# Scoring the edges of a graph attention layer: products on VectorE in place of turned rows on TensorE, and gathers written out

## The reference, cut to what matters

```python
x_l = (x @ W_l + b_l).reshape(n, H, C)          # H = 8 heads of C = 32
x_r = (x @ W_r + b_r).reshape(n, H, C)
src, dst = (edge_index[0], edge_index[1])       # dst is sorted
x_j = x_l[src]
g = jax.nn.leaky_relu(x_r[dst] + x_j, 0.2)
alpha = jnp.einsum('ehc,hc->eh', g, att)        # the scoring stage computes alpha
alpha = alpha + jnp.log(edge_attr)[:, None]
```

## Time and profile before

| | us |
|---|---|
| median of three runs (lowest, highest) | 5924.41 (5920.71, 5925.23) |
| the profiled execution, its own time | 5924.94 |
| its span, first to last instruction | 5923.2 |
| busy: PE, DVE, ACT, POOL | 4048.7, 2628.5, 1112.7, 3097.9 |
| first instruction of the scoring stage | 244.79 |
| first VectorE instruction of the stage after it | 1547.41 |

### The profile page before, as it was taken

How to read it: one execution, slowest core, us unless ns; L and a number is a source line. 1 busy time by engine, 2 the same in 40 slices (tenths; PEclk the granted TensorE clock), 3 DMA queues, 4 the chain that set the end, 5 groups by cost and what they waited for, 6 DMA issues and landing times. The chain is left out here.

```text
span 5923.2 us, 82263 instructions
## 1 busy us (share of the span) xinstructions
PE 4048.7 (68%) x19460; PEld 3300.3 (56%) x19461; DVE 2628.5 (44%) x5923; ACT 1112.7 (19%) x2524; POOL 3097.9 (52%) x3161
## 2 busy tenths in 40 slices
PE   4788999999469965089934555555455555592998
PEld 3577888888447744067734444444444444461665
DVE  5333333333689975034444434444433334342443
ACT  0122222222159921022210000000000000021121
POOL 1166767676248831500066777777677777603111
PEclk9889888888679985599955556666555555555999
DMA  5365555565248843342242111111211111122220
GB/s 197 94 183 182 180 178 181 177 181 177 70 157 273 272 135 108 122 125 64 62 122 54 32 32 33 33 33 30 44 33 32 33 32 34 28 72 81 84 79 31
DMA packets 414884, 602.72 MB, mean 102 GB/s; under 512 B 97612, under 2 KB 305118, under 8 KB 413351
## 3 DMA queue, kind: packets, MB, share of 16 engines
q1 hardware_dynamic: 283019, 348.08, 17.8%
q0 software_dynamic: 107056, 200.91, 14.7%
q10 hardware_dynamic: 24732, 52.87, 2.6%
HBM read 392.17 MB, written 221.97 MB: 104 GB/s over the span
## 5 line engine op out<-in xcount | busy, mean ns | idle before, releaser
L1867 POOL DMA_INDIRECT big<-t_d,src_tiles x1564 | 1497.9, 958 | 552.2 <-issue 462.5
L2090 PE MATMUL v_bank<-big,v_oh 128*128 x3328 | 682.9, 391 | 926.4 <-POOLq L1863 861.6
L2090 PEld LDWEIGHTS v_bank<-big,v_oh 128*128 128x128 f32 x3328 | 649.6, 299 | 1004.0 <-issue 1004.0
L640 POOL DMA_INDIRECT se_xj<-xl_d,se_idx x832 | 833.8, 1002 | 371.9 <-issue 193.0
L1945 DVE TENSOR_TENSOR big<-big,v_bank 128x64 f32 x1664 | 367.8, 221 | 1158.0 <-PE v_bank L2090 922.8
L737 PE MATMUL se_z_ps<-big,se_oht 128*128 x1664 | 543.4, 455 | 73.1 <-issue 45.7
L683 DVE TENSOR_TENSOR se_z<-se_z_ps,se_xj 128x528 f32<-128x528 f32 x416 | 293.3, 705 | 584.8 <-DMA se_xj<-xl_d,se_idx 450.3
L976 POOL TENSOR_TENSOR ae_v<-ae_v,ex 128x1792 f32<-128x1792 f32 x104 | 334.2, 3217 | 243.0 <-DMA ae_v<-xj_d 242.8
L759 PEld LDWEIGHTS se_al_ps<-atta,se_zt 128*128 128x128 f32 x3328 | 459.3, 214 | 0.0
L759 PE MATMUL se_al_ps<-atta,se_zt 128*128 128x8 f32 x3328 | 444.5, 260 | 0.0
L1017 PE MATMUL ae_bank<-ae_v,ae_oh 128*128 128x266 f32 x1664 | 401.1, 396 | 51.4 <-DVE big L1001 37.4
(11 more groups left out here) (406 smaller groups left out, 5916.6 us busy)
## 6 DMA issues: line engine op xcount, KB each, us to landing
xj_d<-se_xj SPq DMA_DIRECT2D x208, 528.0 KB, 3.4
ae_v<-xj_d SPq DMA_DIRECT2D x208, 528.0 KB
big<-t_d,src_tiles POOLq DMA_INDIRECT x1564
buf_d<-e_blank ACTq DMA_DIRECT2D x4, 4112.0 KB, 35.7
e_xs<-buf_d SPq DMA_DIRECT2D x106, 128.0 KB
y_d<-e_y SPq DMA_DIRECT2D x106, 128.0 KB
se_xj<-xl_d,se_idx POOLq DMA_INDIRECT x832, 3.1
v_xt<-xnt_d SPq DMA_DIRECT2D x98, 128.0 KB
```

The costliest lines, as they stand in the source:

```text
L640: nc.gpsimd.indirect_dma_start(half_of(u)[:, k, :], None, table, bass.IndirectOffsetOnAxis(ap=idx[:, u, k:k + 1], axis=0)).then_inc(landed ...
L1867: nc.gpsimd.indirect_dma_start(rows[:, t % RING, :], None, table, bass.IndirectOffsetOnAxis(ap=m.srct[:, t:t + 1], axis=0)).then_inc(lande ...
L2090: last = nc.tensor.matmul(bank[u][:, k * MH:(k + 1) * MH], oh[:, u, k, :], of_block(rows, at[k]), start=True, stop=True)
```

## The change

The scoring stage is rewritten in these parts:

- the leaky ReLU is split as 0.2 z + 0.8 max(z, 0). The folded linear columns take 0.2, and `att` times 0.8 lies in SBUF once for each partition (`attb`).
- VectorE computes w = max(z, 0) * attb for a pair (`weigh`, one instruction of 512 elements a partition), sums w over each head's 32 (`total`, 16 sums), and adds the linear columns once a group.
- TensorE no longer turns z and no longer multiplies by att.
- the one-hots are made on ScalarE, as max(0, 1 - |iota - dl|): eight instructions and one more for a group.
- the turned one-hots have two PSUM tiles in place of one.
- the gathers are written out: no loop, no copy of indices and no wait for it. The index column comes straight from `m.src`.
- the gathered rows lie in the free part of `big1`.

```diff
-        idx = sb("idx", [P, 4, HS], U32)
-        xj = sb("xj", [P, 2, GS, LW])
+        xj = m.big1[:, CL:CL + 2 * GS * LW].rearrange("p (u k d) -> p u k d", u=2, k=GS)
...
-                def gather(h, u, r):
-                    if at_least(h, 4):
+                for h in range(2 * NG):
+                    u, r = h % 4, h // 4
+                    if h >= 4:
                         pool.wait_ge(landed[u], 16 * HS * r)
                         pool.wait_ge(s["z_ready"], 2 * h - 6)
                         pool.wait_ge(stored[u], 16 * r)
-                    nc.gpsimd.tensor_copy(idx[:, u, :], m.src[:, bass.ds(h * HS, HS)]).then_inc(s["indexed"], 1)
-                    pool.wait_ge(s["indexed"], h + 1)
-                    pool.sem_inc(s["issued"], 1)
                     for k in range(HS):
+                        t = h * HS + k
                         nc.gpsimd.indirect_dma_start(half_of(u)[:, k, :], None, table,
-                                                     bass.IndirectOffsetOnAxis(ap=idx[:, u, k:k + 1], axis=0)).then_inc(landed[u], 16)
-                pipeline(pool, 2 * NG, 4, (0, gather))
+                                                     bass.IndirectOffsetOnAxis(ap=m.src[:, t:t + 1], axis=0)).then_inc(landed[u], 16)
...
+                def weigh(q, v, r):
+                    u, k = v // GP, 2 * (v % GP)
+                    dve.wait_ge(s["z_ready"], q + 1)
+                    if at_least(q, 2):
+                        dve.wait_ge(s["totalled"], q - 1)
+                    nc.vector.scalar_tensor_tensor(w[:, v % 2, :, :], z[:, u, k:k + 2, 0:D], 0.0, wide,
+                                                   ALU.max, ALU.mult).then_inc(s["weighed"], 1)
+
+                def total(q, v, r):
+                    dve.wait_ge(s["weighed"], q + 1)
+                    nc.vector.tensor_reduce(m.ex[:, bass.ds(q * 2 * H, 2 * H)],
+                                            w[:, v % 2, :, :].rearrange("p k (h c) -> p (k h) c", h=H), AX.X, ALU.add)\
+                        .then_inc(s["totalled"], 1)
...
+                    dve.wait_ge(s["totalled"], q + 1)
+                    ex = m.ex[:, bass.ds(g * GS * H, GS * H)].rearrange("p (k h) -> p k h", h=H)
+                    nc.vector.tensor_tensor(ex, ex, z[:, u, :, D:LW], ALU.add).then_inc(s["al_ready"], 1)
+                pipeline(dve, NS // 2, 2 * GP, (0, add), (1, weigh), (2, total), (3, scores))
...
+                act.dma_start(attb[:, :], a["L0_gnn_att"].rearrange("h c -> (h c)").partition_broadcast(P)).then_inc(s["att_in"], 16)
...
+                    if at_least(q, 2 * GP):
+                        act.wait_ge(s["oht_made"], 2 * (g - 1))
+                    for k in range(GS):
+                        nc.scalar.activation(oh[:, u, k, :], m.iota[:, :], ACT.Abs, bias=m.dl[:, bass.ds(g * GS + k, 1)],
+                                             scale=-1.0).then_inc(s["oh_apart"], 1)
+                    act.wait_ge(s["oh_apart"], GS * (g + 1))
+                    nc.scalar.activation(oh[:, u, :, :], oh[:, u, :, :], ACT.Relu, bias=m.ones[:, 0:1], scale=-1.0)\
+                        .then_inc(s["oh_ready"], 1)
...
-                pipeline(act, NS // 2, 2 * GP, (0, one_hot_turned), (5, absolute))
+                pipeline(act, NS // 2, 2 * GP, (0, one_hot), (4, one_hot_turned))
...
-                pipeline(pe, NS // 2, 2 * GP, (0, turn_one_hot), (2, expand), (4, turn), (6, attend))
+                pe.wait_ge(s["att_scaled"], 1)
+                pipeline(pe, NS // 2, 2 * GP, (0, turn_one_hot), (2, expand))
```

More of the change, by code:

```diff
@@ L497, in _ @@
                 for q in range(KC):
-                    c.did(nc.vector.tensor_scalar(m.atta[:, q, :], attm[:, q, :], attc[:, q:q + 1], (1 - SLOPE) / 2,
-                                                  ALU.mult, ALU.mult))
-                    c.did(nc.vector.tensor_scalar(attl[:, q, :], attm[:, q, :], attc[:, q:q + 1], (1 + SLOPE) / 2,
+                    c.did(nc.vector.tensor_scalar(attl[:, q, :], attm[:, q, :], attc[:, q:q + 1], SLOPE,
                                                   ALU.mult, ALU.mult))
@@ L616, in score_edges @@
         z = sb("z", [P, 2, GS, LW])
-        zt = sb("zt", [P, 2, 512])
-        oht_ps = ps("oht_ps", [P, 4 * P], BF16)
+        w = sb("w", [P, 2, 2, D])
+        attb = sb("attb", [P, D])
+        oht_ps = [ps(f"oht_ps{i}", [P, 8 * P], BF16) for i in range(2)]
         z_ps = [ps(f"z_ps{i}", [P, 2, 512]) for i in range(2)]
-        zt_ps = [ps(f"zt_ps{i}", [P, 512]) for i in range(2)]
-        al_ps = ps("al_ps", [P, 512])
         s = {n: m.sem("se_" + n) for n in
-             "indexed issued xj0 xj1 xj2 xj3 st0 st1 st2 st3 oh_ready oht_made oht_ready z_made z_ready zt_made zt_ready att_made al_ready keys".split()}
+             "xj0 xj1 xj2 xj3 st0 st1 st2 st3 att_in att_scaled oh_apart oh_ready oht_made oht_ready z_made z_ready weighed totalled al_ready keys".split()}
         landed, stored = [s[f"xj{u}"] for u in range(4)], [s[f"st{u}"] for u in range(4)]
@@ L661, in _ @@
             def _(dve):
[L662 to L671, removed]
+                nc.vector.tensor_copy(identb[:, :], m.ident[:, :]).then_inc(s["att_scaled"], 1)
+                dve.wait_ge(s["att_in"], 16)
+                nc.vector.tensor_scalar(attb[:, :], attb[:, :], 1 - SLOPE, None, ALU.mult).then_inc(s["att_scaled"], 1)
+                dve.wait_ge(s["att_scaled"], 2)
+                wide = attb[:, :].unsqueeze(1).to_broadcast([P, 2, D])
                 def add(q, v, r):
@@ L680, in add @@
                     dve.wait_ge(s["z_made"], q + 1)
-                    if at_least(q, 2 * GP):
-                        dve.wait_ge(s["zt_made"], q - (2 * GP - 1))
                     nc.vector.tensor_tensor(z[:, u, k:k + 2, :], z_ps[v % 2][:, :, 0:LW], xj[:, u, k:k + 2, :],
                                             ALU.add).then_inc(s["z_ready"], 1)
+                def weigh(q, v, r):
[10 more added lines that the diff above has]
+                        .then_inc(s["totalled"], 1)
                 def scores(q, v, r):
@@ L689, in scores, with one_hot @@
                     u, g = v // GP, 2 * r + v // GP
[L690 to L695, removed]
+                    dve.wait_ge(s["totalled"], q + 1)
+                    ex = m.ex[:, bass.ds(g * GS * H, GS * H)].rearrange("p (k h) -> p k h", h=H)
+                    nc.vector.tensor_tensor(ex, ex, z[:, u, :, D:LW], ALU.add).then_inc(s["al_ready"], 1)
+                pipeline(dve, NS // 2, 2 * GP, (0, add), (1, weigh), (2, total), (3, scores))
             @block.scalar
             def _(act):
+                act.dma_start(attb[:, :], a["L0_gnn_att"].rearrange("h c -> (h c)").partition_broadcast(P)).then_inc(s["att_in"], 16)
+                def one_hot(q, v, r):
+                    if v % GP:
+                        return
+                    u, g = v // GP, 2 * r + v // GP
+                    if at_least(q, 2 * GP):
[6 more added lines that the diff above has]
+                        .then_inc(s["oh_ready"], 1)
                 def one_hot_turned(q, v, r):
@@ L705, in one_hot_turned @@
                         act.wait_ge(s["z_made"], GP * (g - 1))
[L706 to L712, removed]
-                pipeline(act, NS // 2, 2 * GP, (0, one_hot_turned), (5, absolute))
+                    nc.scalar.copy(oht[:, u, 4 * half:4 * half + 4, :].rearrange("p k n -> p (k n)"), oht_ps[half][:, 0:4 * P])\
+                        .then_inc(s["oht_ready"], 1)
+                pipeline(act, NS // 2, 2 * GP, (0, one_hot), (4, one_hot_turned))
             @block.tensor
@@ L721, in turn_one_hot @@
                     pe.wait_ge(s["oh_ready"], g + 1)
-                    if at_least(q, 2):
-                        pe.wait_ge(s["oht_ready"], 2 * g + half)
+                    if at_least(q, 2 + 2):
+                        pe.wait_ge(s["oht_ready"], 2 * g + half - 1)
                     for k in range(4):
-                        last = nc.tensor.transpose(oht_ps[:, k * P:(k + 1) * P], oh[:, u, 4 * half + k, :], identb[:, :])
+                        last = nc.tensor.transpose(oht_ps[half][:, k * P:(k + 1) * P], oh[:, u, 4 * half + k, :], identb[:, :])
                     last.then_inc(s["oht_made"], 1)
@@ L2428, in memory @@
     m.tmp0, m.tmp1 = sb("tmp0", [P, NB]), sb("tmp1", [P, NB])
-    m.atta = sb("atta", [P, KC, H])
     m.kvt, m.bd = sb("kvt", [P, KC, P]), sb("bd", [P, KC, P])
```

## The result

| | before | changed |
|---|---|---|
| median of the runs (lowest, highest), us | 5924.82 (5920.71, 5928.17) | 5767.53 (5765.88, 5771.0) |
| ratio, 95% interval | | 0.9739 (0.9723 to 0.9756) |
| span of the profiled execution, us | 5923.2 | 5764.2 |
| scoring, end of the stage before to start of the stage after, us | 243.5 to 1546.9: 1303.4 | 246.2 to 1404.6: 1158.4 |
| one half in steady state, us | 6.013 | 5.338 |

The changed kernel is 157 us faster; 5810 was forecast, in a range of 5725 to 5890. The stage gives 145.0 of the 159.0 us between the two profiled spans. A half is measured here from the first gather after the start-up stand to the end of the last one, divided by 204.

What follows compares the result with a forecast made beforehand. POOL's gather issue was taken as the bound, 6.018 us a half. A half becomes 5.09 + 0.39 = 5.48; 204 x (6.018 - 5.48) = 110, plus 3 at the end and 1 for the first copy: 5811, said as 5810, range 5725 to 5890.

Steps and rivals of the forecast that it cites:

- The bound: Scoring stage: POOL's own issue rate of gathers sets the time, 6.018 us a half.
- The gathers written out: POOL in scoring: copy and wait (0.19 + 0.81 us) go, 0.30 comes instead; a half of 5.02 us.
- The long stands: POOL in scoring: seven idles of 2.04 us instead of 0.30 before a gather, 0.06 a half, assumed to stay.
- The stall of weigh: Scoring: the third gather starts under a running `weigh` and is late by 0.39 us, once a half.
- The size: Whole kernel: 114 us less than 5924.9, so 5811, said as 5810 us.
- the case of one hit: Scoring: one gather a half delayed by `weigh`, 0.39 us; 5785 to 5845 us, chance 0.56.
- The end: After scoring's last gather: the last pairs' work gets shorter, 3 us less, between 0 and 6.
- The first stand: POOL's first stall in scoring (36.09 us), ending with the store of half 0 at 304.19, was to stay.
- VectorE: Scoring: its work takes 3.7 us a half plus about 0.1 for columns, below 5.02, so hidden.
- ScalarE: Scoring: one-hots add at most 4.3 us a group; 7.6 of 10 us with its former work, so hidden.
- TensorE: Scoring: loses two thirds of its instructions; even at the lower clock 5.0 us a half, under 5.47, so hidden.
- The rival in which the gathers hold back VectorE: Scoring: `weigh` waits for gathers, half 6.2 to 6.3, 5980 us; chance 0.09, shared with other VectorE overruns.

Runs made afterwards that it cites:

- e1: Kernel before with only its gathers written out (no loop, index copy, wait or sem_inc), all else as before: 5735.5 us, ratio 0.9690.
- e2: Changed kernel with the gathers put back as they were (loop, index copy, wait for it): 5916.5 us, ratio 0.9981.
- e3: Changed kernel with att times 0.8 in PSUM as two copies, so `weigh` reads one SBUF and one PSUM tensor: 5702.5 us, ratio 0.9635.
- e7: Changed kernel, gathers written out, but index copy, its wait and the sem_inc kept in each half: 5918.3 us, ratio 0.9989.
- e6: Changed kernel with att in PSUM and the 16 sort-key loads spread between SyncE's stores: 5661.7 us, ratio 0.9562.
- e8: e3 with the one-hots made on VectorE again by the comparison, ScalarE's nine instructions taken out: 5730.4 us, ratio 0.9674.
- e9: Changed kernel with VectorE's order add, `total`, `weigh` in place of add, `weigh`, `total`: 5743.6 us, ratio 0.9704.
- e10: e6 with POOL's sem_inc per group of gathers in both convolve stages replaced by a one-column memset: 5675.4 us, ratio 0.9589.
- e4: Changed kernel, gathers written out, with the index copy and its wait kept in each half, without the sem_inc: 5788.2 us, ratio 0.9778.
- e5: Changed kernel with SyncE's 16 sort-key loads spread between its stores instead of ahead of them: 5725.4 us, ratio 0.9664.

## Why the prediction was right, step by step

**The bound** was POOL's issue, as read, and stayed so. e1 and e2 show that all of the gain came from POOL's instructions, and e3 that what the products cost came through the stalled gathers.

**The gathers written out**: 0.71 a half was forecast and came (0.303 in place of 1.01). Its cause was misread. I took the 0.81 for the wait on the copy; 0.27 is that, 0.55 is the sem_inc. The sum held only because the change takes out both. That is luck: had it kept the sem_inc, as e7 does, the same sum would have been over 110 us too fast.

**The long stands** (0.06 a half, 12 us) were kept in the sum and went. They are there with the sem_inc in e2 and e7 and absent in e1, e3 to e6, e8 and e9. In `convolve` they do not depend on it (e10). Nor are they the loading of code: the kernel before has its seven between 451 and 1392 us, and its instruction queues move nothing from 340 to 1530. What they are stays open.

**The stall of weigh**: 0.39 a half forecast, in the third gather; 0.337 measured, in the third gather. The addition came 2.92 instead of 2.97 after the last gather's start, and 11 halves had no long gather. This was the term most in doubt and the only one that speaks against the change. The fourth gather, which the forecast had miss the second `weigh` by 0.05, was long in none.

**The size.** 5810 - 5767.5 = 42.5 us. That lies within the range, but below the 5785 to 5845 that I had given the case of one hit: the rows tell that it was this case, the time alone would not. The stage gave 145.0 us where the forecast had 114. The half came out 0.14 under the forecast of 5.48: 204 x 0.14 = 29, of which the stands are 12, the stall 11, and the gathers' median of 0.947 in place of 0.953 another 5; a half of 6.013 before in place of my 6.018 takes 1 back. The end gave 5.2 instead of 3. The first stand ends 59.5 us into the stage instead of 60.7, 1.2 more. The other 14 of the 159.0 us between the two profiled spans lie in stages that are not touched, for which the forecast had nothing. Of these `finish_attention` gives 6 (114.3 to 108.2 us); its windows, before and after:

```profile
2130.00:2245.00 115.00, 75.08 (x244) 45.34 (x244) 83.37 (x215) 1.53 (x2) 37.71 (x58) 0.86 0.43 123
```

```profile
1989.00:2098.00 109.00, 70.62 (x244) 42.73 (x244) 83.05 (x215) 1.53 (x2) 37.77 (x58) 0.90 0.44 130
```

The granted clock was 0.90 instead of 0.86. e3, e4, e6 and e8 to e10 have the short stage too, e1, e2, e5 and e7 the long one. Why is not settled. `convolve` gives another 5, from its first gather to the end of its last (2023.1 to 2017.9 us).

**VectorE** at 3.7 us a half and a tenth for the columns: its share is 770.54 / 1080 x 5.34 = 3.81. `weigh` 0.681, `total` 0.677. VectorE's idle before additions was forecast at about 1 us a half and is 307 / 204 = 1.5. **ScalarE** and **TensorE** were hidden, as said; TensorE's clock fell from 0.87 to 0.78 and VectorE waited 5 us for it. The rival in which the gathers hold back VectorE found next to nothing: `weigh` is 0.674 to 0.753 long.

## What to carry to other kernels

When POOL issues the gathers that bound a stage, count its own beat first, and among the things between two gathers look for sequencer instructions, which no busy time shows: one sem_inc that nobody waited for was 0.55 us in each half, 112 of this change's 157 us. Then look at which VectorE instructions with two SBUF inputs, and which long copies within SBUF, run as a gather starts. Here one input in PSUM freed the gathers at no cost that shows, and even the order of instructions on VectorE moves the time. A change with several parts wants its parts timed alone: here the gathers gave more than the whole, and the rest cost 30 us.

## What the runs showed of the hardware that I had not expected

- `sem_inc` on POOL, after a wait for POOL's own result: 0.55 us until the next gather starts (0.82 against 0.27 idle).
- The rule of the stall holds from both sides: a gather that starts before the vector instruction is not held (e1: 0.95 with a comparison beginning 0.24 into it); one that starts under it ends 0.82 to 0.83 after it, if two inputs lie in SBUF; with one in PSUM it is not (e3: 147 gathers that start under such a `weigh`, none over 0.957). A copy with one SBUF input, 128x3136 in 1.78 us, holds it too (2.15).
- TensorE at 4.8 us of work in a step of 5.1 was granted 0.99 of its clock; with 5.5 busy in 6.0, 0.87; with a third of the instructions, 0.78.
- 16 broadcasts to eight partitions each, issued ahead of the first rows, kept POOL standing 37.9 us; spread over the stage they cost nothing that can be seen (e6: half 5.000).
